# Value matmuls of two key groups issued in one burst: blocked causal attention inside a transformer layer

## The chip, the core and the metric

The kernel runs on one core of a Trainium2 chip. The core has a matrix engine (TensorE, PE in the profile; its weight loads are shown apart as PEld), a vector engine (DVE), a scalar engine (ACT), a general engine (POOL) and a queue engine (SP) that here only issues transfers. Matrix results are written to PSUM, a memory of eight banks of 128 partitions by 512 float32 words; the working memory is SBUF. Each engine runs its own list of instructions in order, and they meet only by semaphores. The metric is the device time of one execution in microseconds (us); less is better.

## What is computed

One layer over a sequence of 4096 tokens of width 256: causal self-attention of 16 heads of width 16 with rotary positions, a residual and a layer norm, then a three-stage feed-forward net, again with residual and norm. The change touches the attention alone:

```
q, k, v = split_heads(x @ Wq.T + bq), split_heads(x @ Wk.T + bk), split_heads(x @ Wv.T + bv)
q, k = rope(q), rope(k)
att = jnp.einsum('bhqd,bhkd->bhqk', q, k) / sqrt(16)
att = softmax(where(tril, att, -inf), axis=-1)
y   = jnp.einsum('bhqk,bhkd->bhqd', att, v)
x   = layernorm(x + y @ Wo.T + bo)
x   = layernorm(x + ffn(x))
```

## The kernel before

The program has four stages, one after the other: `project` (q, k, v to the chip's main memory), `attend`, `widen` and `narrow` (the feed-forward net). In the profiled execution `attend` begins its matmuls near 190 us and has its last at 1851 us.

**Tiling of the attention.** The heads are taken four at a time (a *quad*, four of them) and the queries 512 at a time (a *chunk*, c = 0 to 7). Quad and chunk make a *block*; the 32 blocks run in the order of `attend_plan` (chunks rising in quads 0 and 2, falling in 1 and 3). q and k are kept as bfloat16 parts stacked to 96 contraction rows, which gives scores of nearly float32 precision in one matmul.

**Row scores.** For each query tile of 128, head and 512 keys, TensorE makes the scores with queries on the partitions (L454, and L457 adds the causal mask on the diagonal). Their only use is the row maximum, which VectorE takes from the bank (`segment`, L531). `row_ps` has 4 banks (`RING_R`), one score tile each: row unit r waits until reduction r-4 is done. When a block's last row unit is reduced, VectorE runs `finish`: five small operations, L538 to L547, that leave the negated maxima as three bfloat16 parts. Four row units later (`TURN_LAG`) a *turn* stands in TensorE's list (L448): a matmul that transposes these parts, which waits for `finish`. SP then stores the result and loads it as 3 further contraction rows of the q stack. There are 32 turns. In all there are 2304 row units and 32 turns.

**Key scores, exponentials, values.** For each *group* (a block and 128 keys, 576 of them) and each of the four heads, TensorE makes the scores the other way round, keys on the partitions, with the maxima subtracted by the 3 extra rows (`key_unit`, L470, mask L473). `key_ps` has 3 banks (`RING_K`): key unit m waits for exponential m-3. ScalarE takes each bank through Exp into `probs` (L595), which has 4 slots of one group (`RING_P`); the exponentials of group g wait for `values(g - 4)`. `values(g)` (L489) waits for the four exponentials of g and multiplies the probabilities with the values of the four heads, 32 columns wide each, so that the four use the four 32-column strips of the array side by side. In float32 each is two matmuls, eight in a group, and their sum over a block's groups gathers in the single bank `at_o`. ScalarE moves it out one group after the block's last (`take_out`, L586), and SP stores it.

**Order on TensorE.** It is written out: for each group and head first the row units that the planner `rows_before_keys` puts there (0 to 10 in a group, most often 4; about one for each key unit, so that the maxima are ready in time), then the key unit; after the fourth key unit of group g, `values(g - 1)`. The first group has 63 row units, and the last 20 groups have key units alone, with a few small pieces of the next stage.

Of the kernel before, what the change touches and what calls it, by code (L numbers as in the profile page):

```python
# [254 lines left out]
def row_width(c, i, s):  # L255
    return CH if s < c else (i + 1) * P


def key_start(c, j):
    return max(0, j * P - c * CH)  # L260
# [29 lines left out]
def attend(nc, io, qp_d, kp_d, v_d, max_d, o_d, front, prep):  # L290
# [3 lines left out]
    NB = len(blocks)  # L294
    NG = len(groups)
    last_row = {n: r for r, (n, i, _, _) in enumerate(rows) if i != TURN}
    turn_at = {n: r for r, (n, i, _, _) in enumerate(rows) if i == TURN}
    last_group = {n: g for g, (n, _) in enumerate(groups)}
    out_after = {min(g + 1, NG - 1): n for n, g in last_group.items()}
    MR = PARTS * QUAD * TPC  # L300
# [4 lines left out]
    with ExitStack() as ctx:  # L305
# [44 lines left out]
        @block.gpsimd  # L350
        def _(pool):
            def load(u, quad):
                q_v = qp_d.rearrange("a (q h d) n t -> a q d h n t", q=NQUAD, d=HD)
                k_v = kp_d.rearrange("a (q h d) n t -> a q d h (n t)", q=NQUAD, d=HD)
                for r, (qa, ka) in enumerate(TERMS):
                    part = slice(r * HD, (r + 1) * HD)
                    for h in range(QUAD):
                        pool.dma_start(qst[u][part, :, h, :], q_v[qa, quad, :, h]).then_inc(stacks_loaded[quad], 16)
                    pool.dma_start(kst[u][part, :, :], k_v[ka, quad]).then_inc(stacks_loaded[quad], 16)

            def load_values(u, quad):
                pool.dma_start(vq[u][:, 0:NT * QUAD * VW], v_d[quad].rearrange("p n i e -> p (n i e)")
                               ).then_inc(values_loaded[quad], 16)

            load_values(0, 0)
            for u in range(2):
                nc.gpsimd.memset(vq[u][:, NT * QUAD * VW:], 0.0).then_inc(pad_ready, 1)  # L367
                pool.wait_ge(pad_ready, u + 1)
                nc.gpsimd.memset(kst[u][SROWS:SROWS + PARTS, :, :], 1.0).then_inc(ones_ready[u], 1)
                pool.wait_ge(ones_ready[u], 1)  # L370
            pool.wait_ge(first_loaded[NCH - 1], 12 * 16)
            load(1, 1)
            load_values(1, 1)
            for quad in range(2, NQUAD):
                pool.wait_ge(probs_used, last_group[(quad - 1) * NCH - 1] + 1)
                load(quad % 2, quad)
                load_values(quad % 2, quad)
            pool.wait_ge(probs_used, last_group[PREP_QUAD * NCH - 1] + 1)
            prep.fill(pool)
            prep.inverse_root(pool, 0)  # L380
# [57 lines left out]
        @block.tensor  # L438
        def _(pe):
            def row_unit(r):  # L440

                n, i, h, s = rows[r]
                if r >= RING_R:
                    pe.wait_ge(rows_taken, r - RING_R + 1)
                bank = row_ps[r % RING_R]
                if i == TURN:
                    pe.wait_ge(maxparts_ready, n + 1)
                    nc.tensor.matmul(bank[0:MR, 0:P], maxparts[:, n % 2, :, :].rearrange("p a r -> p (a r)"), ident[:, :],  # L448
                                     start=True, stop=True).then_inc(rows_ready, 1)
                    return  # L450
                quad, c = blocks[n]
                u = quad % 2
                w = row_width(c, i, s)
                last = nc.tensor.matmul(bank[:, 0:w], qst[u][0:SROWS, c, h, i * P:(i + 1) * P],  # L454
                                        kst[u][0:SROWS, h, s * CH:s * CH + w], start=True, stop=(s < c))
                if s == c:
                    last = nc.tensor.matmul(bank[:, w - P:w], mask[:, :], ident[:, :], start=False, stop=True)  # L457
                last.then_inc(rows_ready, 1)

            def key_unit(g, h):  # L460

                n, j = groups[g]
                quad, c = blocks[n]
                u = quad % 2
                m = QUAD * g + h
                q0 = key_start(c, j)
                if m >= RING_K:
                    pe.wait_ge(probs_ready, m - RING_K + 1)
                bank = key_ps[m % RING_K]
                last = nc.tensor.matmul(bank[:, q0:CH], kst[u][0:SROWS + PARTS, h, j * P:(j + 1) * P],  # L470
                                        qst[u][0:SROWS + PARTS, c, h, q0:CH], start=True, stop=(j < TPC * c))
                if j >= TPC * c:
                    last = nc.tensor.matmul(bank[:, q0:q0 + P], ident[:, :], mask[:, :], start=False, stop=True)  # L473
                last.then_inc(keys_ready, 1)

            def values(g):

                n, j = groups[g]
                quad, c = blocks[n]
                u = quad % 2  # L480
                q0 = key_start(c, j)
                if j == 0 and n > 0:
                    pe.wait_ge(out_taken, n)
                if j == 0 and n % NCH == 0:
                    pe.wait_ge(values_loaded[quad], 16)
                pe.wait_ge(probs_ready, QUAD * (g + 1))
                for h in range(QUAD):
                    at = j * QUAD * VW + h * VW
                    last = nc.tensor.matmul(o_ps[32 * h:32 * h + 32, q0:CH], vq[u][:, at:at + 32],  # L489
                                            probs[:, g % RING_P, h, q0:CH], start=(j == 0), stop=(g == last_group[n]))  # L490
                last.then_inc(probs_used, 1)

            pe.wait_ge(consts_ready, 2)
            pe.wait_ge(pad_ready, 2)
            done = 0
            for g, (n, j) in enumerate(groups):
                for h in range(QUAD):
                    for r in range(done, before[QUAD * g + h]):
                        m, i, head, s = rows[r]
                        if (i, head, s) == (0, 0, 0):  # L500
                            quad, c = blocks[m]
                            if quad == 0:
                                pe.wait_ge(first_loaded[c], 12 * 16)
                            elif m % NCH == 0:
                                pe.wait_ge(stacks_loaded[quad], 30 * 16)
                        row_unit(r)
                    done = before[QUAD * g + h]
                    if j == 0 and h == 0:
                        if n % NCH == 0 and n < 2 * NCH:
                            pe.wait_ge(ones_ready[n // NCH], 1)  # L510
                        pe.wait_ge(max_stored[n % 4], 16 * (n // 4 + 1))
                    key_unit(g, h)
                if g > 0:
                    values(g - 1)
                i = g - rows_done - 4
                if i == 0:
                    pe.wait_ge(rows_taken, len(rows))
                if 0 <= i < TPC:
                    prep.project(pe, 0, i, row_ps[i // 2])
                if i == 12:  # L520
                    prep.turn(pe, 0, row_ps)
            values(NG - 1)

        @block.vector
# [741 lines left out]
```

## Time and profile before

| what | value |
|---|---|
| time, median of 3 runs | 2890.32 us (2888.95 to 2891.99) |
| the profiled execution, its own time | 2888.47 us |
| its span, first to last instruction | 2886.7 us |
| PE busy over the span | 2781.7 us (96%) |
| DVE busy over the span | 1944.8 us (67%) |
| ACT busy over the span | 1296.6 us (45%) |
| mean granted clock of TensorE | 0.984 |

The profile is of one execution. A busy PE is not PE at its peak: matmuls are pipelined and their ends are modelled, so that the shown time of a matmul reaches past the start of the next. What a matmul really takes of the engine is read from start to start. The same holds for DVE and ACT in a row of equal operations: a group "x4" of 2.06 us is three distances from start to start and one whole duration.

### The profile page before, as it was taken

The numbers are of one execution on the slowest core, as the hardware profiler recorded it, in microseconds if no ns is written. First come the engines' busy times: TensorE is split into PE (matmuls) and PEld (weight loads), VectorE is DVE, ScalarE is ACT, GpSimd is POOL, SyncE is SP. The second block draws the span as 40 slices with busy tenths as digits, with TensorE's granted clock in tenths as the row PEclk, the third lists the DMA queues.
The fourth block names the chain that finished last, engine by engine and source line by source line (L and its number), as shares of the span: only waits on it lengthen the run. The fifth ranks groups of instructions, "written<-read, shape, count | busy, mean of one in ns | idle before, by whom it ended". The sixth has DMA issues, their size and how long they took to land. (4 is left out here: it accounts for less than half of the span.)

```text
span 2886.7 us, 39857 instructions
## 1 busy us (share of the span) xinstructions
PE 2781.7 (96%) x15456; PEld 1474.2 (51%) x15456; DVE 1944.8 (67%) x3592; ACT 1296.6 (45%) x2545; POOL 94.8 (3%) x121
## 2 busy tenths in 40 slices
PE   8949999999999999999999999899999999999998
PEld 4423333333333333333333333388888887888887
DVE  7979999988888887888887776353333333344343
ACT  0005666677776676777777777511112111101100
POOL 0030100002000010000000000000000000000000
PEclk9969999999999999999999999999999999999999
DMA  5540270008000017000001000221111132112100
GB/s 155 166 106 27 45 89 3 3 2 103 7 3 4 5 28 91 3 3 3 3 3 38 18 4 8 75 71 56 57 59 64 48 124 111 44 44 87 44 15 23
DMA packets 94569, 132.89 MB, mean 46 GB/s; under 512 B 30688, under 2 KB 68192, under 8 KB 90688
## 3 DMA queue, kind: packets, MB, share of 16 engines
q1 hardware_dynamic: 83184, 96.91, 10.4%
q0 software_dynamic: 5472, 23.34, 6.5%
q10 hardware_dynamic: 5744, 10.36, 1.2%
q8 instruction: 110, 1.80, 0.3%
q14 instruction: 59, 0.48, 0.1%
HBM read 83.25 MB, written 47.32 MB: 45 GB/s over the span
## 5 line engine op out<-in xcount | busy, mean ns | idle before, releaser
L531 DVE TENSOR_REDUCE at_segmax<-at_row 128x1 f32<-128x512 f32 (+3 forms) x2304 | 1329.1, 638 | 236.2 <-PE at_row L454 178.3
L595 ACT ACTIVATE at_probs<-at_key 128x512 f32<-128x512 f32 (+3 forms) x2304 | 1130.9, 567 | 532.6 <-PE at_key L470 362.3
L454 PE MATMUL at_row<-fr_k_stack,fr_q_stack 96*128 96x512 bf16 (+3 forms) x1152 | 407.3, 374 | 32.2 <-POOL at_values L367 28.3
L470 PE MATMUL at_key<-fr_q_stack,fr_k_stack 99*128 99x512 bf16 (+3 forms) x1152 | 414.7, 364 | 2.7 <-ACT at_probs L595 2.7
L454 PE MATMUL at_row<-at_k_stack,at_q_stack 96*128 96x512 bf16 (+3 forms) x1152 | 412.1, 364 | 1.4 <-DVE at_segmax L531 1.2
L470 PE MATMUL at_key<-at_q_stack,at_k_stack 99*128 99x512 bf16 (+3 forms) x1152 | 402.8, 364 | 6.7 <-ACT at_probs L595 6.2
L489 PE MATMUL at_o<-at_probs,at_values 128*32 128x512 f32 (+3 forms) x2304 | 286.9, 570 | 0.0
L489 PE MATMUL at_o<-at_probs,fr_values 128*32 128x512 f32 (+3 forms) x2304 | 286.4, 569 | 0.0
L454 PEld LDWEIGHTS at_row<-fr_k_stack,fr_q_stack 96*128 96x128 bf16 x1152 | 112.1, 99 | 309.2 <-DVE at_segmax L531 202.1
L454 PEld LDWEIGHTS at_row<-at_k_stack,at_q_stack 96*128 96x128 bf16 x1152 | 112.0, 97 | 293.2 <-DVE at_segmax L531 211.1
L1128 ACT ACTIVATE na_h3f<-na_h,na_hs 128x512 f32<-128x512 f32 x64 | 44.1, 690 | 401.9 <-PE na_h L1098 401.9
L1098 PE MATMUL na_h<-na_h_h,fr_h2w_h 128*128 128x512 f32 x512 | 203.7, 398 | 5.4 <-DVE na_h_l L1143 5.4
L1098 PE MATMUL na_h<-na_h_l,fr_h2w_h 128*128 128x512 f32 x512 | 203.4, 397 | 0.0
L1098 PE MATMUL na_h<-na_h_h,fr_h2w_l 128*128 128x512 f32 x512 | 203.4, 397 | 0.0
L897 PE MATMUL wi_f<-wi_h_h,wi_h1w_h 128*128 128x512 f32 x512 | 201.4, 393 | 0.0
L897 PE MATMUL wi_f<-wi_h_l,wi_h1w_h 128*128 128x512 f32 x512 | 199.3, 389 | 0.0
L897 PE MATMUL wi_f<-wi_h_h,wi_h1w_l 128*128 128x512 f32 x512 | 199.3, 389 | 0.0
L1150 DVE CAST na_h_h<-na_h3f 128x512 fp32r<-128x512 f32 x64 | 27.3, 427 | 245.8 <-ACT na_h3f L1128 245.8
L941 ACT ACTIVATE wi_h<-wi_f,fr_hs 128x512 f32<-128x512 f32 x64 | 44.1, 689 | 324.6 <-PE wi_f L897 324.6
L470 PEld LDWEIGHTS at_key<-at_q_stack,at_k_stack 99*128 99x128 bf16 x1152 | 111.6, 98 | 146.9 <-ACT at_probs L595 78.8
L897 PE MATMUL wi_f<-fr_x1t,fr_w_h 128*128 128x512 f32 x512 | 160.8, 396 | 9.1 <-PEq L305 9.0
L470 PEld LDWEIGHTS at_key<-fr_q_stack,fr_k_stack 99*128 99x128 bf16 x1152 | 112.8, 98 | 94.7 <-ACT at_probs L595 27.8
(125 smaller groups left out, 2702.7 us busy)
## 6 DMA issues: line engine op xcount, KB each, us to landing
hidden<-wi_h SPq DMA_DIRECT2D x64, 256.0 KB, 2.0
na_h2f<-hidden SPq DMA_DIRECT2D x8, 1024.0 KB, 8.4
q_parts<-pr_parts SPq DMA_DIRECT2D x48, 128.0 KB, 1.9
k_parts<-pr_parts SPq DMA_DIRECT2D x48, 128.0 KB, 2.2
at_q_stack<-q_parts POOLq DMA_DIRECT2D x48, 128.0 KB, 23.8
at_k_stack<-k_parts POOLq DMA_DIRECT2D x12, 512.0 KB, 27.7
values<-pr_vals SPq DMA_DIRECT2D x32, 136.0 KB, 2.8
outputs<-at_outs SPq DMA_DIRECT2D x128, 34.0 KB
```

The costliest lines, as they stand in the source:

```text
L454: last = nc.tensor.matmul(bank[:, 0:w], qst[u][0:SROWS, c, h, i * P:(i + 1) * P], kst[u][0:SROWS, h, s * CH:s * CH + w], start=True, stop= ...
L470: last = nc.tensor.matmul(bank[:, q0:CH], kst[u][0:SROWS + PARTS, h, j * P:(j + 1) * P], qst[u][0:SROWS + PARTS, c, h, q0:CH], start=True, ...
L489: last = nc.tensor.matmul(o_ps[32 * h:32 * h + 32, q0:CH], vq[u][:, at:at + 32], probs[:, g % RING_P, h, q0:CH], start=(j == 0), stop=(g = ...
L531: nc.vector.tensor_reduce(segmax[:, n % 2, h * TPC + i, s:s + 1], row_ps[r % RING_R][:, 0:w], op=ALU.max, axis=AX.X).then_inc(rows_taken, 1)
L595: nc.scalar.activation(probs[:, g % RING_P, h, q0:CH], key_ps[m % RING_K][:, q0:CH], ACT.Exp).then_inc(probs_ready, 1)
L897: last = nc.tensor.matmul(bank[:, :], w[a][:, c, cols], moving(b, c), start=(m == 0), stop=(m == 3 * count - 1))
L941: nc.scalar.activation(h2[:, k % 2, :], fb[k % 4][:, :], ACT.Gelu, scale=front.hs[:, k:k + 1]).then_inc(hid_taken, 1)
L1098: last = nc.tensor.matmul(hb[k % 4][:, :], h2w[a][:, c, cols], h2[b][:, c, :], start=(m == 0), stop=(m == 3 * FK - 1))
L1128: nc.scalar.activation(h3f[:, k % 2, :], hb[k % 4][:, :], ACT.Gelu, scale=hs[:, k:k + 1]).then_inc(hid_taken, 1)
L1150: nc.vector.tensor_copy(h3[0][:, k, :], h3f[:, k % 2, :]).then_inc(h3_high, 1)
```

## The change

`values` is called for two groups at once: nothing is issued after an odd group, and after an even group g stand `values(g - 2)` and `values(g - 1)` one behind the other. At the end `values(NG - 2)` joins `values(NG - 1)`. The banks, rings and all other orders stay as they are: the row banks stay single, four of them.

```
                     key_unit(g, h)
-                if g > 0:
+                if g % 2 == 0 and g > 0:
+                    values(g - 2)
                     values(g - 1)
                 i = g - rows_done - 4
...
+            values(NG - 2)
             values(NG - 1)
```

The first place is TensorE in quad 1, around the turn of its chunk-6 block (`at_row` is a row unit, `at_key` a key unit, `at_o` a values burst, L448 the turn). Before:

```order
L489 MATMUL at_o<-at_probs,fr_values 32x512 x4
L454 MATMUL at_row<-at_k_stack,at_q_stack 128x512
L470 MATMUL at_key<-fr_q_stack,fr_k_stack 128x512
L454 MATMUL at_row<-at_k_stack,at_q_stack 128x512
L470 MATMUL at_key<-fr_q_stack,fr_k_stack 128x512
L454 MATMUL at_row<-at_k_stack,at_q_stack 128x512
L448 MATMUL at_row<-at_ident,at_maxparts 48x128
L470 MATMUL at_key<-fr_q_stack,fr_k_stack 128x512
L454 MATMUL at_row<-at_k_stack,at_q_stack 128x512
L470 MATMUL at_key<-fr_q_stack,fr_k_stack 128x512
L489 MATMUL at_o<-at_probs,fr_values 32x512 x4
```

The same place in the changed program:

```order
L454 MATMUL at_row<-at_k_stack,at_q_stack 128x512
L470 MATMUL at_key<-fr_q_stack,fr_k_stack 128x512
L454 MATMUL at_row<-at_k_stack,at_q_stack 128x512
L470 MATMUL at_key<-fr_q_stack,fr_k_stack 128x512
L454 MATMUL at_row<-at_k_stack,at_q_stack 128x512
L448 MATMUL at_row<-at_ident,at_maxparts 48x128
L470 MATMUL at_key<-fr_q_stack,fr_k_stack 128x512
L454 MATMUL at_row<-at_k_stack,at_q_stack 128x512
L470 MATMUL at_key<-fr_q_stack,fr_k_stack 128x512
L489 MATMUL at_o<-at_probs,fr_values 32x512 x8
```

The burst that stood between the block's last row unit and its turn is gone; it now stands behind the turn, with the next one.

The second place is TensorE in quad 0, in a full stretch where the planner puts nine row units beside eight key units; these rows are the changed program's, from just after one burst to the next. Before, a burst stood in their middle, behind the fourth key unit:

```order
L454 MATMUL at_row<-fr_k_stack,fr_q_stack 128x512 x2
L470 MATMUL at_key<-fr_q_stack,fr_k_stack 128x512
L454 MATMUL at_row<-fr_k_stack,fr_q_stack 128x384
L457 MATMUL at_row<-at_ident,at_mask 128x128
L470 MATMUL at_key<-fr_q_stack,fr_k_stack 128x512
L454 MATMUL at_row<-fr_k_stack,fr_q_stack 128x512
L470 MATMUL at_key<-fr_q_stack,fr_k_stack 128x512
L454 MATMUL at_row<-fr_k_stack,fr_q_stack 128x512
L470 MATMUL at_key<-fr_q_stack,fr_k_stack 128x512
L454 MATMUL at_row<-fr_k_stack,fr_q_stack 128x512
L470 MATMUL at_key<-fr_q_stack,fr_k_stack 128x512
L489 MATMUL at_o<-at_probs,fr_values 32x512 x8
```

Row and key units keep their order among themselves; only the bursts are moved.

## Rows read from the trace of the kernel before

**Rows 1.** Busy time of each engine in the attention, 240 to 1853 us.

```profile
core 0: us, PE busy (x) PEld busy (x) DVE busy (x) ACT busy (x) POOL busy (x), PEclk, DMA share, GB/s
...
240.00:1853.00 1613.00, 1588.16 (x10103) 542.34 (x10102) 1334.70 (x2429) 1133.83 (x2318) 49.86 (x95) 1.00 0.14 22
```

**Rows 2.** PE in order of time: start, duration, what; a steady group of quad 1.

```profile
905.14 0.38 PE L470 MATMUL at_key<-at_q_stack,at_k_stack 99*128 99x512 bf16 x1
905.45 1.07 PE L489 MATMUL at_o<-at_probs,at_values 128*32 128x512 f32 x8
906.45 0.39 PE L454 MATMUL at_row<-at_k_stack,at_q_stack 96*128 96x512 bf16 x1
906.67 0.38 PE L470 MATMUL at_key<-at_q_stack,at_k_stack 99*128 99x512 bf16 x1
```

**Rows 3.** The same view at the end of attention: two bursts alone, then two together, with ACT and PEld.

```profile
1841.58 0.64 PE L489 MATMUL at_o<-at_probs,at_values 128*32 128x256 f32 x8
1842.15 1.09 PE L757 MATMUL at_row<-fr_ident,fr_x 128*128 128x128 f32 x8
...
1844.64 0.43 PE L489 MATMUL at_o<-at_probs,at_values 128*32 128x128 f32 x8
1845.00 0.34 PE L470 MATMUL at_key<-at_q_stack,at_k_stack 99*128 99x384 bf16 x1
...
1850.58 0.60 ACT L595 ACTIVATE at_probs<-at_key 128x128 f32<-128x128 f32 x2
...
1850.80 0.86 PE L489 MATMUL at_o<-at_probs,at_values 128*32 128x256 f32 x16
1851.23 0.16 PEld L489 LDWEIGHTS at_o<-at_probs,at_values 128*32 128x32 f32 x8 [0.28 <-ACT at_probs L595]
```

**Rows 4.** ACT and DVE in order of time around the burst of Rows 2.

```profile
904.74 1.57 ACT L595 ACTIVATE at_probs<-at_key 128x512 f32<-128x512 f32 x3
...
906.87 2.48 DVE L531 TENSOR_REDUCE at_segmax<-at_row 128x1 f32<-128x512 f32 x4 [0.56 <-PE at_row L454]
...
907.15 2.07 ACT L595 ACTIVATE at_probs<-at_key 128x512 f32<-128x512 f32 x4 [0.84 <-PE at_key L470]
```

**Rows 5.** Costliest groups of the page: busy, mean ns, idle before and its releaser.

```profile
L531 DVE TENSOR_REDUCE at_segmax<-at_row 128x1 f32<-128x512 f32 (+3 forms) x2304 | 1329.1, 638 | 236.2 <-PE at_row L454 178.3
L595 ACT ACTIVATE at_probs<-at_key 128x512 f32<-128x512 f32 (+3 forms) x2304 | 1130.9, 567 | 532.6 <-PE at_key L470 362.3
```

**Rows 6.** DVE and PE around the turn of the first order piece.

```profile
711.17 1.89 DVE L531 TENSOR_REDUCE at_segmax<-at_row 128x1 f32<-128x512 f32 x3 [0.36 <-PE at_row L454]
713.09 0.27 DVE L538 TENSOR_REDUCE at_negmax<-at_segmax 128x16 f32<-128x112 f32 x1
...
714.02 0.17 DVE L547 TENSOR_TENSOR at_maxparts<-at_maxrest,at_maxparts 128x16 bf16<-128x16 f32 x1
...
714.53 0.38 PE L454 MATMUL at_row<-at_k_stack,at_q_stack 96*128 96x512 bf16 x1
714.85 0.24 PE L448 MATMUL at_row<-at_ident,at_maxparts 128*48 128x128 bf16 x1
```

**Rows 7.** PE at a turn with no burst between it and the last row.

```profile
880.04 0.38 PE L454 MATMUL at_row<-at_k_stack,at_q_stack 96*128 96x512 bf16 x1
881.47 0.24 PE L448 MATMUL at_row<-at_ident,at_maxparts 128*48 128x128 bf16 x1 [1.04 <-DVE at_segmax L531]
```

**Rows 8.** PE's two longest pauses, and granted clock (PEclk) in stretches behind them.

```profile
1134.57 0.39 PE L470 MATMUL at_key<-fr_q_stack,fr_k_stack 99*128 99x512 bf16 x1 [1.74 <-ACT at_probs L595]
...
1136.20:1139.50 3.30, 3.30 (x10) 1.06 (x8) 2.78 (x5) 1.79 (x3) 0.00 (x0) 0.50 0.05 18
...
1798.18 0.22 PE L448 MATMUL at_row<-at_ident,at_maxparts 128*48 128x128 bf16 x1 [1.92 <-DVE at_maxparts L547]
...
1798.40:1801.60 3.20, 3.20 (x12) 0.52 (x12) 0.28 (x1) 2.06 (x4) 0.00 (x0) 0.50 0.10 23
```

More of the change, by code:

```diff
@@ L512, in _ @@
                     key_unit(g, h)
-                if g > 0:
+                if g % 2 == 0 and g > 0:
+                    values(g - 2)
                     values(g - 1)
@@ L521, in _ @@
                     prep.turn(pe, 0, row_ps)
+            values(NG - 2)
             values(NG - 1)
```

## The prediction

> **What bounds the kernel now.** I read the busy time by engine for the attention first, then the matrix engine in order of time, then who waits for it. In the attention PE is busy 1588 of 1613 us at a clock of 1.00 [rows 1], and the order of time shows why: row and key matmuls of 512 columns start 0.22 us apart (906.45 to 906.67 [rows 2]) and one burst of values follows another with hardly a hole. DVE and ACT both end their idle time on TensorE's scores [rows 5], so they are the followers. But DVE is a close one: it is busy 1335 of the 1613 us [rows 1].
>
> What the change attacks is the price of entering and leaving a burst. The last key matmul starts at 905.14 and would let go at 905.36; the burst starts at 905.45, so 0.09 to 0.10 us go on the way in. From there the next matmul starts at 906.45, 1.00 us later [rows 2]. Eight matmuls of 512 columns in two waves of four would take some 0.85 us if a wave costs two 512-column matmuls (2 x 2 x 0.213, an estimate from the 0.22 us spacing), so 0.15 us go on the way out.
>
> **What a joined burst saves.** The trace has one: the last two bursts of the attention stand together, 256 and 128 columns wide, 0.86 us of busy time [rows 3]. Alone they run 0.57 us (1841.58 to 1842.15) and 0.36 us (1844.64 to 1845.00) to the next matmul, and their shown 0.64 and 0.43 us reach 0.07 us past that. The pair thus takes 0.86 - 0.07 = 0.79 us where 0.57 + 0.36 + 0.10 for the second entry = 1.03 us would stand: 0.235 us saved. The pair's second half even had to wait for ACT, whose last exponential ended at 1851.18, and loads its weights at 1851.23. So the saving is no less than 0.235 us here; I take it for all widths, since entry and exit do not depend on the width. There are 576 bursts and 288 pairs, one of them joined already: 287 x 0.235 = 67 us, if nothing else moves. The instructions stay the same in number, and no wait on ACT is added: key unit 3 of group g has already waited for the first exponential of g, which is later than all those of g - 1. Block borders fall between pairs, as every block has a multiple of four groups, and the fourth probs slot is free in time: the values of g - 4 still end a whole group before the exponentials of g want it.
>
> **What it costs.** The row and key units now come in runs of eight and more, and their rings of four and three banks were only ever tested with runs of four. I walk one run, time 0 at its first row unit, from these terms: DVE starts 0.42 us after an idle start (906.45 to 906.87), reduces every 0.60 us (x4 of 2.48 less x3 of 1.89), one whole reduction is 0.69 us; ACT starts 0.48 us after its key (906.67 to 907.15), an exponential every 0.49 us, a whole one 0.59 us [rows 2, 4, 6]; a release costs 0.05 us (1851.18 to 1851.23 [rows 3]).
>
> - Row unit m may start at 1.16 + 0.60 (m - 4), key unit m at 1.34 + 0.49 (m - 3). Eight rows, eight keys: row 7 may start at 2.96 and would at 3.08; key 7 may at 3.30 and would at 3.30. It fits with nothing to spare. In the joined burst of 1.95 us both followers drain. Uneven places of the rows cost some 0.06 us: gain 0.17 us.
> - Nine rows: row 8 may start at 3.56 and would at 3.36. With 0.15 us of wait on the mean the gain is 0.08 us.
> - Ten rows or more: row 9 waits 0.30 us (4.16 against 3.86), and DVE's 0.42 + 10 x 0.60 = 6.4 us no longer fit in the 6.0 us of PE's run and burst, so that 0.4 us is carried into the next run. Before, a burst after every five rows gave DVE its time. Walked over both, a loss of 0.28 us.
> - Runs on a diagonal, with narrow keys and many narrow rows: the same walk over two of them gives 0 and 0.15 us of gain. I take 0.07 us; the ends of the other cases, 0.235 gain and 0.28 loss, are its bounds.
>
> **The turns.** This is the term that the diff does not show. A turn needs the block's last reduction (0.6 us), the small operations (713.09 to 714.11, with the start of the next about 1.1 us) and, for its bank, the reduction of the row unit after the last (0.68 us). Before, TensorE gets to it 1.8 us of row and key units later, plus one burst: at 714.75 it could go, at 714.85 it goes [rows 6]. Where no burst stands between, it is 1.04 us of pause, even with narrow units [rows 7]. In the order 9 of the 32 turns have no burst between the last row unit and the turn before, and 23 after. So 14 more turns pay some 1.1 us (the 1.04 of rows 7, and the 1.00 of the missing burst plus the 0.1 already waited): 15.4 us. Their runs have nine to fifteen row units as well and pay for these like the long runs, 30 x 0.2 = 6 us, and they get the saving, 30 x 0.235 = 7 us. Net 14.4 us over 30 runs, 0.48 each.
>
> **The sum.** Between the first and the last burst the changed order has 285 runs: 95 full ones with up to eight row units (-0.17 each: -16.2 us), 45 with nine (-3.6), 31 with ten or more (+8.7), 84 on a diagonal (-5.9), 30 with a turn (+14.4). That is -2.6 us of the 67. To it I add the clock. Twice PE paused for over 1.6 us in the attention (1.74 and 1.92 us), and both times it ran at half clock (0.50, 1.2 of 2.4 GHz) for some 3.3 us right after [rows 8], a loss of 1.7 us each. The new pauses at turns are 1.1 to 1.7 us long. I take one such fall more, +1.7 us. In all -0.9 us on a span of 2886.7 us, 2885.8; the profiled run took 1.8 us more than its span and stood 1.8 us under the median, so 2889.4 us for a median: I say 2889.
>
> **Rivals.**
> *DVE keeps up, the saving stays.* If the reductions ran at 0.59 us or the turns cost half, 7 to 10 us more come off: 2880 us. With no new wait at all it is 67 us less, 2823. For it: DVE is idle 236 us before L531 [rows 5]. Against: that idle time lies behind bursts, where it cannot be used twice. 16% for the first, 2% for the second.
> *The clock falls at the turns.* This one ends on the slow side. 23 turns would now pause PE, and a pause of 1.7 us was enough before. From four falls beyond those of now the time is over 0.2% longer; with twelve it is 20 us more, 2909 us. Against: the 1.04 us pause of [rows 7] did nothing, as the clock of the whole stretch rounds to 1.00 [rows 1]. 20%.
> *Weight loads show.* A joined burst could have to load its second set of weights in the open, 0.16 us each [rows 3]: 287 x 0.16 = 46 us more, 2935 us. The pair in the trace speaks against it: its loads begin at 1851.23 and no 0.16 us is missing from its 0.86. 2%. The Trainium skill has this as a rule (TensorE: Matmul & The Clock Gate, Part 3: weight loads overlap running matmuls only where the row group differs, and here all use the full height); by that rule this rival would be the result, and the trace does not agree.
> *It does not do what it says.* The order shows 224 bursts of eight and 64 pairs of unequal width standing together, and no wait lies between them. Under 1%.
>
> The Trainium skill has also a rule for the change (TensorEngine Tiling, Key Properties: a change of tiling mode drains the engine); it gives no price, and the 0.24 us of [rows 2] is what it would be here.
>
> **How the numbers follow.** 60% for the forecast, 18% for faster, 22% for slower. A change under 0.2%, 5.8 us, cannot be told from none here. My forecast lies close to zero as a difference of large terms: a hundredth of a microsecond more in a reduction is worth some 3 us in the long runs, and turns at 0.9 in place of 0.48 us are worth 12. The range runs from 2880 (the first rival) to 2904 (turns at their upper price, or eight falls of the clock). Faster by over 0.2%: 0.19; within: 0.58; slower: 0.23.
>
> **What would show it.** Right: entries before L489 halved in number and joined bursts of 1.95 us; the idle time of PE ahead of L454 and L448 up by some 50 us in sum, with DVE L531 as releaser, and with L448 alone at some 30 us; PE's busy time down by about as much as its idle time is up. In a steady run with eight rows two groups take 5.5 in place of 5.7 us. Wrong: a hole inside a joined burst, PE idle ahead of L470 for ACT in steady runs, or more than three stretches at clock 0.50. If the blocks of quad 0 are not slower than before (there the planner puts the most rows), the ring of four was not the cost.

## The result and the profile after

| | kernel before | changed kernel |
|---|---|---|
| median | 2889.12 us (8 runs, 2887.93 to 2894.09) | 2900.51 us (8 runs, 2896.33 to 2905.93) |
| ratio, 95% interval | | 1.0037 [1.0026, 1.0048] |
| profiled execution: time, span | 2888.47, 2886.7 us | 2896.33, 2894.5 us |
| mean granted clock of TensorE | 0.984 | 0.982 (0.978 to 0.982 over the runs, 0.980 on the mean) |

The change costs 11 us, 0.4%. The time lies in the range, but the likeliest case was no change, and that is wrong: it is slower by more than the measurement's uncertainty. The profiled execution is the fastest of the eight, so it shows the loss at its smallest.

The last row of the table already says where to look. Time lost to the clock is the span times what the clock lacks to 1: 0.016 x 2887 = 46 us before, 0.020 x 2900 = 58 us after, 12 us more. That is as large as the loss, within the rounding of the clock. It is a pointer and no proof yet: the sum also counts time at half clock in which TensorE had nothing to do. It does not hang on one execution: the runs of the kernel before that stand beside the experiments have a clock of 0.983 to 0.985, those of the changed kernel 0.978 to 0.982.

First the joined burst, PE in order of time in the changed kernel (start, duration, what):

```profile
906.64 1.71 PE L489 MATMUL at_o<-at_probs,at_values 128*32 128x512 f32 x16
908.28 0.39 PE L454 MATMUL at_row<-at_k_stack,at_q_stack 96*128 96x512 bf16 x1
...
911.04 0.86 PE L489 MATMUL at_o<-at_probs,at_values 128*32 128x256 f32 x16
911.83 0.34 PE L454 MATMUL at_row<-at_k_stack,at_q_stack 96*128 96x384 bf16 x1
```

These two are of mixed widths (512 with 384, and 256 with 128). The second takes 0.79 us to the next matmul, just as the one pair of [rows 3] did. From all starts in the trace, the 224 pairs of 512 with 512 columns take 1.857 us (median) to the next matmul, where two single bursts with an entry between took 2 x 0.998 + 0.096 = 2.092 us: 0.235 us saved, as forecast. The number of bursts in the attention falls from 574 to 287 (all but the last burst, which was a joined one before too). The saving is there: 67 us.

Then what it costs. A long run, PE in order of time in quad 0, where the row ring of four banks holds TensorE back:

```profile
395.18 0.38 PE L470 MATMUL at_key<-fr_q_stack,fr_k_stack 99*128 99x512 bf16 x1
395.46 0.39 PE L454 MATMUL at_row<-fr_k_stack,fr_q_stack 96*128 96x512 bf16 x1
396.06 0.39 PE L454 MATMUL at_row<-fr_k_stack,fr_q_stack 96*128 96x512 bf16 x1 [0.21 <-DVE at_segmax L533]
...
397.19 1.92 PE L489 MATMUL at_o<-at_probs,fr_values 128*32 128x512 f32 x16
```

The second row unit starts 0.60 us after the first in place of 0.22: that is VectorE's pace of one reduction.

Then the turn of the first order piece, to be held against [rows 6]:

```profile
724.71 0.38 PE L454 MATMUL at_row<-at_k_stack,at_q_stack 96*128 96x512 bf16 x1
724.93 0.22 PE L457 MATMUL at_row<-at_ident,at_mask 128*128 128x128 bf16 x1
...
726.52 0.38 PE L454 MATMUL at_row<-at_k_stack,at_q_stack 96*128 96x512 bf16 x1
727.94 0.24 PE L448 MATMUL at_row<-at_ident,at_maxparts 128*48 128x128 bf16 x1 [1.04 <-DVE at_segmax L533]
```

Before, PE went from the last row unit ahead of this turn to the turn in 0.32 us (714.53 to 714.85); now in 1.42 us. The waits of PE behind its own matmuls, first before, then after (view of the waits, attention alone: us in total, times, longest):

```profile
PE at_row L448 <- DVE at_segmax L531: 8.0, 12, 1.4
PE at_row L454 <- DVE at_segmax L531: 2.9, 10, 0.4
```

```profile
PE at_row L448 <- DVE at_segmax L533: 21.7, 20, 1.4
PE at_row L454 <- DVE at_segmax L533: 9.7, 40, 0.4
```

This view counts a wait only from the modelled end of the last matmul. From start to start, the waits ahead of row units and turns rise from 35.0 to 82.3 us, those ahead of key units from 30.3 to 48.6 us. Together 66 us more: the saving of 67 us is used up almost to the last microsecond, as the forecast had it.

And the clock. The granted clock, PEclk, is the number after the five busy columns:

```profile
core 0: us, PE busy (x) PEld busy (x) DVE busy (x) ACT busy (x) POOL busy (x), PEclk, DMA share, GB/s
252.30:255.50 3.20, 3.20 (x16) 0.50 (x16) 0.91 (x3) 0.60 (x1) 0.00 (x0) 0.50 0.04 9
853.10:856.30 3.20, 3.20 (x15) 0.53 (x8) 0.48 (x2) 0.00 (x0) 0.00 (x0) 0.50 0.02 5
948.60:951.80 3.20, 3.20 (x14) 0.72 (x18) 0.64 (x4) 0.60 (x1) 0.00 (x0) 0.50 0.04 9
993.00:996.20 3.20, 3.20 (x14) 0.92 (x16) 2.07 (x5) 1.54 (x3) 0.00 (x0) 0.50 0.04 8
1150.00:1156.70 6.70, 6.34 (x23) 2.01 (x27) 3.19 (x5) 4.16 (x8) 0.00 (x0) 0.50 0.06 23
1808.80:1812.00 3.20, 3.20 (x12) 0.72 (x16) 0.00 (x0) 2.80 (x6) 0.00 (x0) 0.50 0.11 26
```

Six stretches of the attention at 1.2 in place of 2.4 GHz (called falls from here on), 23.8 us in all, where there were two of 3.4 us each [rows 8]. One of them close up, PE in order of time:

```profile
990.50 0.39 PE L454 MATMUL at_row<-fr_k_stack,fr_q_stack 96*128 96x512 bf16 x1
992.15 0.24 PE L448 MATMUL at_row<-at_ident,at_maxparts 128*48 128x128 bf16 x1 [1.26 <-DVE at_segmax L533]
992.32 0.39 PE L470 MATMUL at_key<-at_q_stack,at_k_stack 99*128 99x512 bf16 x1
992.75 0.49 PE L454 MATMUL at_row<-fr_k_stack,fr_q_stack 96*128 96x512 bf16 x1
993.03 0.63 PE L470 MATMUL at_key<-at_q_stack,at_k_stack 99*128 99x512 bf16 x1
993.46 0.31 PE L454 MATMUL at_row<-fr_k_stack,fr_q_stack 96*128 96x128 bf16 x1
```

A turn waits, and under a microsecond after it the same matmul of 512 columns is shown with 0.63 us in place of 0.38, the next starting 0.43 us later in place of 0.22. The first four stretches follow such a turn. Two of these turns (near 851 and 992 us) had a burst ahead of them before; the other two (near 251 and 948 us) waited as long before, with no fall. So only 6.8 of the 17.0 us that came on top stand behind waits that the joining laid bare. The fall at 1150 lies at a wait for a transfer, the last one follows the same turn as before.

### The profile page after: what moved, and what is told of

Read it like the earlier page. It is cut to its first block and busy times, and to the rows that moved or that the text cites. A ratio compares the mean times of both kernels' runs of the same rounds, so it can differ in the third digit from the quotient of the medians.

```text
span 2894.5 us, 39857 instructions
## 1 busy us (share of the span) xinstructions
PE 2764.4 (96%) x15456; PEld 1500.5 (52%) x15456; DVE 1926.0 (67%) x3592; ACT 1282.2 (44%) x2545; POOL 94.6 (3%) x121
## 5 line engine op out<-in xcount | busy, mean ns | idle before, releaser
L533 DVE TENSOR_REDUCE at_segmax<-at_row 128x1 f32<-128x512 f32 (+3 forms) x2304 | 1309.8, 636 | 262.4 <-PE at_row L454 199.3
L597 ACT ACTIVATE at_probs<-at_key 128x512 f32<-128x512 f32 (+3 forms) x2304 | 1111.0, 579 | 549.0 <-PE at_key L470 374.7
L454 PE MATMUL at_row<-fr_k_stack,fr_q_stack 96*128 96x512 bf16 (+3 forms) x1152 | 414.0, 375 | 38.4 <-POOL at_values L367 28.2
L470 PE MATMUL at_key<-fr_q_stack,fr_k_stack 99*128 99x512 bf16 (+3 forms) x1152 | 415.4, 364 | 4.9 <-ACT at_probs L597 4.7
L470 PE MATMUL at_key<-at_q_stack,at_k_stack 99*128 99x512 bf16 (+3 forms) x1152 | 408.3, 366 | 7.9 <-ACT at_probs L597 4.8
L489 PE MATMUL at_o<-at_probs,at_values 128*32 128x512 f32 (+3 forms) x2304 | 260.5, 570 | 0.0
L489 PE MATMUL at_o<-at_probs,fr_values 128*32 128x512 f32 (+3 forms) x2304 | 259.2, 568 | 0.0
L470 PEld LDWEIGHTS at_key<-at_q_stack,at_k_stack 99*128 99x128 bf16 x1152 | 111.3, 97 | 174.2 <-ACT at_probs L597 116.5
L470 PEld LDWEIGHTS at_key<-fr_q_stack,fr_k_stack 99*128 99x128 bf16 x1152 | 112.3, 98 | 109.7 <-ACT at_probs L597 55.5
```

Source lines behind the costliest of these rows:

```text
L533: nc.vector.tensor_reduce(segmax[:, n % 2, h * TPC + i, s:s + 1], row_ps[r % RING_R][:, 0:w], op=ALU.max, axis=AX.X).then_inc(rows_taken, 1)
L597: nc.scalar.activation(probs[:, g % RING_P, h, q0:CH], key_ps[m % RING_K][:, q0:CH], ACT.Exp).then_inc(probs_ready, 1)
```

## The experiments

All kernels differ from the changed kernel or from the one before in a few lines. Theory A: the joined bursts save what they should, the row ring and the turns give it back, and the clock that falls behind turn pauses makes the net loss. Its rivals: the joined burst itself is at fault (theory B), or the waits alone are and the clock has no part.

**Joined everywhere but at the turns.** `values(g - 2)` is joined only where `joined(g)` holds; else each burst stands as before.

```
+            def joined(g):
+                run = rows[before[QUAD * (g - 1) - 1]:before[QUAD * g + QUAD - 1]]
+                return all(i != TURN for _, i, _, _ in run)
...
                 if g % 2 == 0 and g > 0:
-                    values(g - 2)
+                    if joined(g):
+                        values(g - 2)
                     values(g - 1)
+                elif g % 2 == 1 and g + 1 < NG and not joined(g + 1):
+                    values(g - 1)
```

> The changed kernel, but the two bursts are not joined in the 31 runs that hold a turn; 257 pairs stay joined. Theory A (the joined bursts lay bare the waits at the turns, and behind these pauses the clock of TensorE falls): the pauses of over 0.7 us in the attention go back from about 24 to about 10, the falls to half clock from 6 to 1 to 3, and the time to 2870 to 2873 us, 17 us or more under the kernel before, since the other pairs keep their saving. Theory B (the joined burst itself is what is slow or lowers the clock, wherever it stands): 257 of 287 parts of the loss stay, 2898 to 2900 us, with five or more falls.

Measured 2874.85 us, ratio to the kernel before 0.9945 [0.9928, 0.9961]; three falls in the attention, 10.2 us; 9 pauses of over 0.7 us. That is 2 us above my upper figure. The trace has 258 joined bursts and 60 single ones, so 30 pairs are split and not the 31 of the expectation. Splitting these 30 of 288 pairs turns 11 us of loss into 16 us of gain. Theory B falls: the other joined bursts do no harm on balance. One of the three falls, near 252 us, stands behind a turn with a pause of 1.55 us that is not joined here.

**The complement: joined at the turns alone.** The condition is turned round, `any(i == TURN ...)`.

> The complement of the kernel that splits at the turns: only the 31 pairs whose run holds a turn are joined, the other 257 are split as before. Theory A (waits at turns, then the clock): by the walk the waits alone cost 17 us less the saving of 31 joins, 13 to 17 us in all, and the new falls of the clock 5 to 9 us on top, so 2905 to 2914 us, slower than the changed kernel with all pairs joined. If the turns were not the place, 31 of 287 joins could move the time by 2 us at most: 2889 us.

Measured 2914.07 us, 1.0085 [1.0069, 1.01], with six falls, 27.2 us at half clock; the time is at the upper end of what was expected. 30 joins (31 joined bursts in the trace, one of them joined before too) cost 23 us; it is slower than the kernel that joins all. In the prediction the 30 runs with a turn were to cost 14 us.

**TensorE kept at work in the pauses.**

```
+            def keep_busy(m):
+                if m >= RING_K:
+                    pe.wait_ge(probs_ready, m - RING_K + 1)
+                    for _ in range(16):
+                        nc.tensor.matmul(key_ps[m % RING_K][:, 0:P], ident[:, :], ident[:, :], start=True, stop=True)
...
+                        if i == TURN and since >= TURN_LAG + 1:
+                            keep_busy(QUAD * g + h)
```

(`since` counts the row units since the last burst.)

> The changed kernel with 16 matmuls of 128 columns more (a constant by itself, into the key bank that is next in turn and is overwritten after) ahead of each of the 20 turns that have no burst between them and the block's last row unit. They fill about 0.9 us of a wait of 1.1 to 1.7 us, and nothing waits less. Theory A: the wait for VectorE stays, the falls of the clock in the attention go from 6 to 1 to 3, and the time to 2891 to 2894 us although TensorE has more to do. If the waits alone cost the time and the clock nothing: 2900 us as in the changed kernel, or more.

Measured 2893.31 us over 10 runs, 1.0008 [0.9999, 1.0018], clock 0.982 to 0.984. The same turn as in the last fence, PE in order of time:

```profile
986.63 0.39 PE L454 MATMUL at_row<-fr_k_stack,fr_q_stack 96*128 96x512 bf16 x1
986.86 1.06 PE L497 MATMUL at_key<-at_ident 128*128 128x128 bf16 x16
988.29 0.24 PE L448 MATMUL at_row<-at_ident,at_maxparts 128*48 128x128 bf16 x1 [0.37 <-DVE at_segmax L544]
988.46 0.39 PE L470 MATMUL at_key<-at_q_stack,at_k_stack 99*128 99x512 bf16 x1
988.89 0.39 PE L454 MATMUL at_row<-fr_k_stack,fr_q_stack 96*128 96x512 bf16 x1
989.12 0.38 PE L470 MATMUL at_key<-at_q_stack,at_k_stack 99*128 99x512 bf16 x1
```

The turn still comes 1.66 us after the row unit ahead of it (986.63 to 988.29; 1.65 in the changed kernel), so the wait is the same; but PE worked for some 0.9 us of it, and the matmuls behind keep their 0.38 us. No fall follows any of the 20 filled turns. 320 more matmuls and 7 us less time than the changed kernel: the clock's part is shown, and "the waits alone" falls. Against the kernel before the time is the same. Three falls are left, 17.0 us: at the transfer wait, behind the last turn, and one at 1833 us with no pause of over 0.7 us just ahead of it.

**Half the reductions.** `row_ps[r % RING_R][:, 0:w]` becomes `[:, 0:w // 2]` in L531, in the kernel before and in the changed one. Each maximum is then taken over half of its scores: another stabilising number for the softmax, the same work elsewhere.

> The kernel before, but each row maximum is taken over the first half of its columns alone (the softmax then subtracts another number), so that a reduction of 512 columns takes some 0.33 in place of 0.60 us. It is the partner of the next. Theory A: the row ring hardly waits any more (14 in place of 48 us by the walk): 2855 us. If VectorE were never in the way: 2889 us.

> The changed kernel with the same half reductions. Theory A (VectorE's ring eats the saving of the joined bursts): against the kernel with half reductions and single bursts it is 40 to 48 us faster, at 2812 us, 44 by the walk with 67 as the saving and the rest lost to waits for ScalarE. Theory B (a joined burst saves little, for instance because its second weight loads show): within 10 us of the kernel with half reductions and single bursts.

Measured 2865.38 us (0.9912 [0.9895, 0.9928]) with single bursts and 2827.84 us (0.9785 [0.9769, 0.9802]) with joined ones. Joining now gains 37.5 us, a little less than the 40 expected, where it lost 11. The first came out 10 us above its expectation; the waits ahead of row units went from 35.0 to 15.9 us where I had expected 14 from 48, so the walk had begun with too much wait. The second came out 16 us above the 2812 expected. Of what halving gains, some 5 us lie ahead of the first key unit and so not in the table below. The busy times of the attention, single then joined (a line of the busy time view each):

```profile
240.00:1831.00 1591.00, 1574.75 (x10061) 541.65 (x10059) 910.43 (x2409) 1126.17 (x2308) 49.87 (x95) 1.00 0.14 22
```

```profile
240.00:1793.00 1553.00, 1525.47 (x10063) 578.67 (x10055) 902.28 (x2406) 1104.43 (x2307) 49.67 (x95) 1.00 0.15 23
```

DVE (third column) is at 910 of 1591 us in place of 1335 of 1613 [rows 1]. So VectorE's pace decides whether joining all bursts pays.

**Joined only where it pays.** The condition becomes `len(run) <= 9 and all(i != TURN ...)`: no turn and at most nine row units between two bursts, 217 pairs. The second kernel of the two has `TURN_LAG = 5` as well.

> Joined only where the run of two groups holds no turn and at most nine row units: 217 pairs. Theory A with the row ring as the second price: the runs of ten and more give 4 us against the kernel that splits at the turns alone (by the walk 12 us), so 2859 to 2868 us. If only turns mattered and long runs cost nothing, 40 joins fewer would make it 9 us slower than that kernel, 2884 us.

> The same selection, and each turn stands five row units behind its block's last in place of four, so that its waits shrink. By the walk 2 us less than with four, 2857 to 2866 us, with no more falls of the clock; if the turns' waits are covered already, the same.

Measured 2865.6 us, 0.9914 [0.9901, 0.9928], and 2863.72 us, 0.991 [0.9896, 0.9923]. Forty joins fewer than in the kernel split at the turns gain 9 us more, so the runs of ten and more row units were a loss. Both times lie in what was expected. The 2 us of the later turn are less than the runs can tell, as the two intervals overlap; in the trace its turn waits fall from 15.1 to 8.8 us and its attention takes 1607.1 in place of 1610.1 us, both with 17.0 us at half clock. Both are faster than the two kernels of this study, by 25 and 27 us against the one before.

**The changed kernel again.**

> The changed kernel unchanged, for a second profile and on the chip of the others: 2896 to 2906 us, mean clock 0.978 to 0.982 against 0.984 before, with five or more falls in the attention of which most follow a turn's pause. If the falls of the first profile were chance, the clock here is 0.984.

Measured 2902.19 us, 1.0044 [1.0029, 1.006], clock 0.978 to 0.981; eight falls in the attention, 34.0 us, six of them behind a turn's pause of 1.2 to 1.55 us, five of these at turns whose wait the joining has laid bare or made longer. That there are more falls is no chance of one execution, but which turns they follow changes: of 21 turn pauses over 0.7 us (the last turn aside) four were followed by one in the first profile and six in this one. The sixth is the turn near 251 us. Its pause of 1.55 us stands in the kernel before as well, with no fall. A fall follows it in all six profiles of kernels with full reductions and bursts joined by the change where the pause is not filled, also in those that leave this turn's run single; why is open.

The two profiles also give the price of a fall directly. Five blocks have 3.4 us more at half clock in one of them than in the other, and take 1.3 to 1.7 us longer with it; the blocks with no fall in either differ by 0.02 us at most.

**The account of all.** For each profile: from the first to the last start in the attention's key and value matmuls, the sums of the waits from start to start, and the time at half clock, all worked out from every PE start in the trace.

| kernel | attention, us | joins x 0.235 | row and turn waits | key waits | at half clock |
|---|---|---|---|---|---|
| before | 1632.3 | 0 | 35.0 | 30.3 | 6.8 |
| changed | 1638.6 | 67.4 | 82.3 | 48.6 | 23.8 |
| changed, again | 1643.5 | 67.4 | 82.6 | 49.2 | 34.0 |
| PE busy at turns | 1635.0 | 67.4 | 64.5 | 48.1 | 17.0 |
| split at turns | 1617.5 | 60.4 | 61.5 | 46.9 | 10.2 |
| turns alone joined | 1657.5 | 7.1 | 56.5 | 33.2 | 27.2 |
| at most nine rows, no turn | 1610.1 | 51.0 | 41.0 | 47.9 | 17.0 |
| half reductions, single | 1613.5 | 0 | 15.9 | 29.7 | 10.2 |
| half reductions, joined | 1574.5 | 67.4 | 22.5 | 49.7 | 13.6 |

To close the account I take half of the time at half clock as lost, which is an upper bound: where PE waits in it, nothing is lost. For the changed kernel: -67.4 + 47.3 + 18.3 + 8.5 = +6.7 us, and the trace has +6.3. For the half reductions: -67.4 + 6.6 + 20.0 + 1.7 = -39.1, and it has -39.0. For the selection: -51.0 + 6.0 + 17.6 + 5.1 = -22.3, and it has -22.2. For the kernel with filled pauses (its 320 matmuls at 0.055 us are 17.7 us): -67.4 + 29.5 + 17.8 + 5.1 + 17.7 = +2.7, and it has +2.7. The others close less well: +12.7 against +11.2 for the changed kernel again, -15.6 against -14.8 for the split at the turns, +27.5 against +25.2 for the turns alone, and -18.0 against -18.8 for the half reductions with single bursts. So the account is good to some 2 us, and a line of it is not finer than that. Of the 7.9 us between the spans of the first two profiles 6.3 lie in the attention; nearly all of the rest lies ahead of the first key matmul (219.1 and 220.9 us), where no burst was moved.

## Why the prediction was wrong

- **The saving of a joined burst** (0.235 us, 67 us in all): right, 0.235 us measured on 224 pairs. No weight load shows, so that rival is out, and with it the rule that a weight load overlaps running matmuls only where the row group differs (the Trainium skill, TensorE: Matmul & The Clock Gate, Part 3): with a load of 0.16 us in the open a pair would save 0.075 us. The same part of the Trainium skill also lets a load into the background weight buffer go ahead of running matmuls, which the prediction left out. The hidden loads fit that.
- **The walks over the rings:** right in their sum. At full clock the attention takes 1632.3 - 3.4 = 1628.9 us before and 1638.6 - 11.9 = 1626.7 us after, 2.2 us less where the walks and turns gave 2.6; the second profile gives 1626.5. That the two agree so closely is in part luck, since the 2.2 hold 1.8 us of a wait for a transfer (below) that was not foreseen. By kind of run, from the waits ahead of row, key and turn units in both traces: a run with up to eight rows gains 0.17 us, with nine 0.07 (0.11 without the transfer), on a diagonal 0.07, and one with ten or more loses 0.26, where the walks gave 0.17, 0.08, 0.07 and 0.28. The sign "PE idle ahead of L470 for ACT in steady runs" did come, small: in runs with up to eight rows the key units wait 0.07 us more in each run, where the walk had put 0.06 for uneven places. The blocks of quad 0, chunks 2 to 4, are slower by 1.9, 2.8 and 2.6 us with no fall in them, and those of chunk 7 faster by 0.8 to 1.9, as the ring would have it.
- **The turns** (14 more without a burst ahead, 1.1 us each): right in place and price. The turn waits rise from 15.4 to 29.6 us, 14.2 where I had 15.4. All in all a run with a turn loses 0.43 us where I had 0.48.
- **The clock** (+1.7 us, "one such fall more"): this is the step that failed. The time at half clock rose by 17.0 us in the profile that stands in the comparison and by 27.2 in the second, at most 8.5 and 13.6 us lost where the forecast had 1.7. I had reasoned from a pause of 1.04 us that did nothing, and from two of over 1.6 us that did, and put the new pauses of 1.1 to 1.5 us, all but one, with the harmless. In its place: of the 21 turn pauses over 0.7 us, new and old, 4 and 6 were followed by a fall. The mechanism was on the list, at 20%, with "from four falls beyond those of now" as the point from which it decides; it got four and six beyond, with one fall of 6.8 us in the first profile and two in the second. Filling the pauses took the falls away at all 20 turns and 7 us off the time, so this term is shown and not only argued.
- **Part of it was not foreseen:** at the block of quad 2, chunk 3, PE waits for ScalarE, which waits to reuse its output tile until SP's stores have gone, while POOL's loads for the next quad are under way. The wait was 1.74 us before [rows 8] and is 3.70 in the changed kernel:

```profile
1149.22 0.60 ACT L588 ACTIVATE at_outs<-at_o 128x512 f32<-128x512 f32 x1 [4.03 <-DMA outputs<-at_outs]
...
1150.36 0.61 PE L470 MATMUL at_key<-fr_q_stack,fr_k_stack 99*128 99x512 bf16 x1 [3.70 <-ACT at_probs L597]
```

  It is 2 us of wait and a fall of 6.8 in place of 3.4 us, so some 3.7 of the 8 us between the two profiles. From start to start it is 3.0 and 2.5 us in the two kernels that keep most bursts single, and 3.6 to 5.0 in the others, against 1.9 in the one profile of the kernel before. Ahead of it SP is held for long in issuing one store of the maxima (`maxima<-at_maxrows`), which else takes 0.31 us: 13.0 us before, 13.5 and 14.4 in those two kernels, 15.2 to 16.5 in the seven others. So in all ten profiles the longer wait goes with joining most bursts; why the issue takes longer was not tried.
- **The sign:** with terms of 67 and 66 us against each other, the net hung on the smallest term. The bound of 2904 us held the median, though not each run (up to 2905.93); the likeliest value was wrong in sign.

## What to carry to other kernels

A batch of work on the bounding engine is only as cheap as the rings beside it are deep: before joining two pieces, walk one run with the follower's pace and see which unit would wait, and look for a rare unit (here one in 73) whose latency the old order happened to cover. Join where the walk leaves room, and leave the order alone elsewhere: that made of a loss of 11 us a gain of 25. A new pause on TensorE can cost more than its length, so count each pause of more than a microsecond as one that may halve the clock for some microseconds behind it.

## What the runs showed of the hardware

- The granted clock falls to 0.50 for about 3.4 us, at times 6.8, behind pauses of 1.1 to 1.55 us in otherwise dense matmuls, but not behind each: none of eight turn pauses of over 0.7 us in the one profile of the kernel before (the last turn, 2.09 us, or 1.82 with half reductions, was followed by one in every profile), four and six of 21 in the two of the changed kernel. With sixteen matmuls of 128 columns in the pause no fall followed any of 20 turns. A fall of 3.4 us cost 1.3 to 1.7 us.
- In three kernels one fall (at 1833 us with PE busy at turns, near 1807 and 1805 in the two selections) has no pause of over 0.7 us right ahead; it lies where only key units are left and PE waits for ScalarE again and again.
- Bursts of four 32-column float32 matmuls side by side follow one another without a hole, on the same column strips: 1.857 us for two of 512 columns. What a joined burst saves is the changeover from and to full-width matmuls: 0.096 us in (the last key matmul to the burst, beyond its own spacing) and 2 x 0.998 - 1.857 = 0.14 us out.
